# Three reorderings in a seven-stage transformer kernel: weight cracking, key tiles, and a scaling on GpSimd

## The chip, the cores and the metric

One core of a Trainium2 chip runs the whole program in one launch. TensorE (PE) multiplies matrices, VectorE (DVE) and ScalarE (ACT) do element-wise work and reductions, GpSimd (POOL) does the rest of the element-wise work, and SyncE (SP) issues the transfers. The engines run their own instruction lists in order and wait for each other through semaphores. The metric is the device time of the launch in microseconds (us), lower is better.

## What is computed

The input x is 2 batches of 1024 tokens with 256 channels, float32. Seven blocks with a residual connection follow each other; each normalises x first. Cut to what the change touches:

```python
x = x + softcap_attention(layernorm(x))       # 16 heads of 32, tanh softcap
x = x + relu_ffn(layernorm(x))                # 256 -> 512 -> 512 -> 256, the first time
x = x + plain_attention(layernorm(x))         # 16 heads of 16, 4 key heads
x = x + relu_ffn(layernorm(x))                # same weights, the second time
x = x + differential_attention(layernorm(x))  # below
x = x + gated_ffn(layernorm(x))               # weights packed as 4-bit codes with scales
x = x + test_time_training_attention(layernorm(x)); x = x + gated_ffn(layernorm(x))

# relu_ffn
x = relu(x @ W1.T + b1); x = relu(x @ W2.T + b2); out = x @ W3.T + b3
# plain_attention: causal softmax
attn = softmax(where(causal, q @ k.T / sqrt(16), min)); y = attn @ v
# differential_attention: two softmaxes, the second one scaled, and a softmax of the difference
s = softmax(where(later, -1e30, energy) / 4)
diff = where(later, -1e30, s[0] - lam * s[1]); att = softmax(diff) @ v
# unpacking of the gated feed-forward's weights
low, high = W & 15, W >> 4 & 15; W = LUT[stack(low, high)] * scales
```

## The kernel before

The stages run one after another; each of them is a function with one instruction list per engine. x (2048 tokens by 256) stays in on-chip memory. Three stages matter here.

**The small feed-forward** (`relu_ffn`, L917) runs twice, as f2 and f4, with the same weights. It works in four blocks of 512 tokens (i = 0 to 3). Float32 products are made of three products of rounded parts: each operand is held as a high part and a remainder, "low". For a block, TensorE runs `second(i)`, `first(i + 1)`, `third(i)` in this order (L1079 ff.): `first` gives the four 512-wide tiles of the first layer, `second` those of the second, `third` the output, which VectorE adds to x in `add(i)` (L1136, line L1140). ScalarE writes high parts and whole values of each tile (`relu`), and VectorE writes the remainder (`remainder`, L1128, line L1132). TensorE's `second(i)` may start only once `add(i - 1)` has emptied the accumulator bank it writes. Numbering the tiles of a block by j, tiles 0 to 3 belong to the first layer and 4 to 7 to the second.

Beside this, the stage unpacks ("cracks") the 4-bit weights of a later gated feed-forward, which have nothing to do with its own result. A part of the weights takes four VectorE steps, `crack(step)` (L955): two shifts with a mask into `f_bits` (L964, L967), an "or" into `f_code` (L971), and the multiplication by the scales into `f_weight` (L977). There are eight parts, so 32 steps, in one stage. ScalarE rounds a finished part (`keep_high`, L985), GpSimd subtracts the rounded from the whole (`keep_low`, L990), and a transfer stores it. GpSimd also adds the bias b3 to x (`add_bias`, L1011). One crack step stands behind each remainder from the third on (L1133), the last two behind the loop (L1163).

**The plain attention** (`attention` with `plain=True`, L492; tiles named ab_ and fb_) works in eight groups of one batch and four heads (g). A group has 12 steps: query block 0 (512 queries) against key tiles 0 to 3 of 128 keys, query block 1 against key tiles 0 to 7, in rising order (`steps`, L535). On the diagonal a tile needs fewer queries: tile kt of block qb is 512 wide where it lies wholly before the block, and 512, 384, 256 and 128 wide for the four diagonal tiles. `pipelined` (L402) makes the list of each engine: in slot u it issues every operation of the list with its own lag, that is for unit u - lag. On TensorE slot u holds four pieces of row scores for the running maxima (`row_piece`, L606; their widths repeat every three slots), with the scores of step u - 15 (`scores`, L634, four heads, two and two) and the weighing of the values of step u - 17 (`weigh`, L656, four heads) in between. VectorE takes the maximum of each row piece (L801); three accumulator banks rotate, so TensorE can be at most three pieces ahead. ScalarE takes the exponentials of the scores (L719), and GpSimd sets the later keys of a diagonal tile to zero (`drop_later`, L763). At the end of a group's rows the maxima are turned (`turn_maxima`, L619), split in three parts on VectorE and transferred into `fb_q_st` (L587); the scores of the group's first step wait for that transfer.

The slots of a group are named below by k = u mod 12, so the scores in slot k are those of step (k + 9) mod 12, and the weighing is that of step (k + 7) mod 12. The maxima are turned at the start of slot k = 1; the first step's scores stand in slot k = 3.

**The differential attention** (`diff_attention`, L1337; tiles named ad_) has 256 units, one for a row block of 128 queries and one head. In the 32 units of a group the row blocks t = 0 to 7 rise, four heads each, and a row of block t is (t + 1) * 128 keys wide. "Short rows" are t = 0 to 3. In slot u GpSimd issues `spread_top` of unit u - 4 (L1539), `mask` of unit u (L1522, waits for the first exponentials of unit u), and `scale_second` of unit u - 2 (L1531, waits for the coefficient of its pair of units). VectorE issues the row maxima of unit u (L1566), `mix` of unit u - 3 (L1595, waits for mask and scaling of its unit), and for every second unit the coefficients of unit u - 1.

## Time and profile before

| what | us |
|---|---|
| median of three runs | 2919.26 |
| lowest and highest of them | 2914.34, 2929.24 |
| the profiled execution's own time | 2915.69 |
| its span in the profile | 2914.0 |
| mean granted TensorE clock | 0.918 of full speed |

| stage | from, to in the span, us |
|---|---|
| first small feed-forward (f2) | 443.5 to 565 |
| plain attention (ab) | 670 to 1017 |
| second small feed-forward (f4) | 1017.5 to 1139 |
| differential attention (ad) | 1234 to 1945 |

The span is the time from the first to the last instruction of one profiled execution; what lies around it is 1.7 us. The trace gives for every instruction its start and duration, the idle time of its engine before it, and what ended that idle time. TensorE's granted clock is 1.00 at 2.4 GHz and 0.50 at 1.2 GHz. Busy times of TensorE include the latency of pipelined products, so a busy TensorE need not be at its peak.

### The profile page before, as it was taken

What the parts mean: (1) busy time and instruction counts of PE and PEld (TensorE: products, weight loads), DVE (VectorE), ACT (ScalarE), POOL (GpSimd) and SP (SyncE); (2) the same over time, 40 slices, a digit from 0 to 9 for tenths busy, and PEclk for the clock granted to TensorE, in tenths of its full rate; (3) what the DMA queues carried; (4) which work ended last, traced back from release to release, by engine and by line L of the source; (5) the groups of instructions that cost most, each with busy time, mean ns of one, the idle gap of its engine ahead of it and who ended that gap; (6) DMA issues with size and microseconds to landing.
All of it is one profiled execution on the core that took longest, in us unless ns stands there. A gap on an engine that the chain in (4) does not pass through costs nothing. (4 is left out here: it accounts for less than half of the span.)

```text
span 2914.0 us, 68812 instructions
## 1 busy us (share of the span) xinstructions
PE 2469.1 (85%) x25231; PEld 1667.2 (57%) x25320; DVE 1960.1 (67%) x4292; ACT 1710.9 (59%) x3452; POOL 856.4 (29%) x1233
## 2 busy tenths in 40 slices
PE   8887878788888788888888888878999687899998
PEld 4433336643333276445555555557888466888898
DVE  5488886667787466698888888874333355566652
ACT  2588874324454453388788788853332334677778
POOL 2244332121111121255555555520000222232223
PEclk9999888878999889999999999989999777899999
DMA  4533302244243022522140222004000658622210
GB/s 173 156 80 79 72 7 72 87 115 59 38 50 45 1 78 96 142 25 31 16 46 2 31 31 30 2 7 174 1 1 2 105 140 158 101 30 33 43 35 8
DMA packets 280879, 175.04 MB, mean 60 GB/s; under 512 B 204768, under 2 KB 241136, under 8 KB 278512
## 3 DMA queue, kind: packets, MB, share of 16 engines
q1 hardware_dynamic: 271392, 162.45, 26.7%
q10 hardware_dynamic: 9168, 8.41, 1.2%
q8 instruction: 192, 3.15, 0.5%
q14 instruction: 127, 1.04, 0.1%
HBM read 111.75 MB, written 54.66 MB: 57 GB/s over the span
## 5 line engine op out<-in xcount | busy, mean ns | idle before, releaser
L1481 ACT ACTIVATE ad_e<-ps,ad_nm 128x1024 f32<-128x1024 f32 (+7 forms) x512 | 380.2, 744 | 113.0 <-DVE ad_nm L1566 107.8
L1566 DVE TENSOR_REDUCE ad_nm<-ps 128x1 f32<-128x1024 f32 (+7 forms) x512 | 372.1, 752 | 43.8 <-PE ps L1414 31.5
L719 ACT ACTIVATE ab_e<-ps 128x512 f32<-128x512 f32 (+3 forms) x384 | 167.0, 490 | 194.9 <-PE ps L634 194.0
L1412 PE MATMUL ps<-fd_k_st,fd_q_st 96*128 96x512 bf16 (+3 forms) x768 | 215.9, 341 | 56.8 <-ACT ad_e L1481 51.2
L1595 DVE CUSTOM_DVE_ANT_0 ad_t<-ad_e,ad_rz 128x128 f32<-128x128 f32 (+7 forms) x256 | 208.2, 813 | 41.3 <-POOL ad_e L1531 24.1
L1531 POOL TENSOR_SCALAR ad_e<-ad_e,ad_c 128x128 f32<-128x128 f32 (+7 forms) x256 | 191.9, 749 | 19.3 <-DVE ad_c L1583 17.8
L1427 PE MATMUL ps<-ident,ad_t 128*128 128x128 f32 x1152 | 170.9, 276 | 26.3 <-ACT ad_prT L1491 12.7
L2007 POOL TENSOR_TENSOR st_it_low<-st_it,st_it_high 128x256 fp32r<-128x256 f32 x128 | 98.5, 783 | 315.2 <-ACT st_it_high L2270 309.7
L1491 ACT ACTIVATE ad_prT<-ps 128x128 f32<-128x128 f32 (+7 forms) x256 | 166.3, 650 | 21.4 <-PE ps L1435 21.3
L1522 POOL TENSOR_SCALAR_AFFINE_SELECT ad_e<-ad_e 128x128 f32<-128x128 f32 x256 | 90.7, 354 | 299.6 <-ACT ad_e L1481 274.4
L724 ACT ACTIVATE aa_e<-ps 128x1024 f32<-128x1024 f32 (+1 forms) x192 | 150.3, 824 | 38.0 <-PE ps L634 35.3
L840 DVE TENSOR_TENSOR aa_e_sum<-aa_e_sum,aa_e 128x2048 f32<-128x2048 f32 (+3 forms) x80 | 150.4, 1880 | 21.5 <-POOL aa_e L775 18.6
L775 POOL TENSOR_TENSOR aa_e<-aa_e,keep 128x512 f32<-128x512 f32 x64 | 108.8, 1706 | 185.4 <-ACT aa_e L731 185.2
L606 PE MATMUL ps<-fb_k_row,fb_q_row 96*128 96x512 bf16 (+3 forms) x384 | 127.4, 376 | 35.3 <-DVE ab_nm_two L801 23.8
L634 PE MATMUL ps<-fa_q_st,fa_k_st 96*128 96x512 f32 (+3 forms) x384 | 125.5, 421 | 34.1 <-ACT aa_e L724 32.3
L1427 PEld LDWEIGHTS ps<-ident,ad_t 128*128 128x128 f32 x1152 | 143.4, 143 | 17.9 <-issue 1.6
L801 DVE TENSOR_REDUCE ab_nm_two<-ps 128x1 f32<-128x512 f32 (+3 forms) x256 | 134.1, 580 | 15.7 <-PE ps L609 10.9
L731 ACT ACTIVATE aa_e<-aa_e 128x2048 f32<-128x2048 f32 (+1 forms) x96 | 143.8, 1499 | 0.0
L634 PEld LDWEIGHTS ps<-fa_q_st,fa_k_st 96*128 96x128 f32 x384 | 64.8, 207 | 137.7 <-ACT aa_e L724 83.9
L1435 PE MATMUL ps<-ad_top_diag,ad_minus 128*128 128x512 f32 (+3 forms) x384 | 133.6, 402 | 7.8 <-POOL ad_top_diag L1539 7.1
L1412 PEld LDWEIGHTS ps<-fd_k_st,fd_q_st 96*128 96x128 bf16 x768 | 56.7, 100 | 145.0 <-ACT ad_e L1481 117.0
L763 POOL TENSOR_SCALAR_AFFINE_SELECT ab_e<-ab_e 128x512 f32<-128x512 f32 x64 | 40.6, 634 | 326.9 <-ACT ab_e L719 326.9
(383 smaller groups left out, 7096.0 us busy)
## 6 DMA issues: line engine op xcount, KB each, us to landing
scr_a<-pa_parts SPq DMA_DIRECT2D x24, 512.0 KB, 2.7
fa_q_st<-scr_a SPq DMA_DIRECT2D x24, 512.0 KB, 7.8
split<-f_split SPq DMA_DIRECT2D x16, 768.0 KB, 3.9
fd_q_st<-scr_d SPq DMA_DIRECT2D x48, 256.0 KB, 8.0
g_w<-split SPq DMA_DIRECT2D x8, 1536.0 KB, 17.8
scr_d<-pd_parts SPq DMA_DIRECT2D x20, 384.0 KB, 2.8
st_w_first<-split ACTq DMA_DIRECT2D x5, 1536.0 KB, 8.1
fa_k_st<-scr_a SPq DMA_DIRECT2D x24, 256.0 KB, 8.5
```

What stands on the lines that cost most here:

```text
L634: last = pe.matmul(m.ps[:, bank, lo:QB], k_st[:, par, h // share, kt * P:(kt + 1) * P], q_st[:, par, h, qb * QB + lo:(qb + 1) * QB], start ...
L719: act.activation(e[:, u % ER, h, lo:QB], m.ps[:, n4(u, h) % 3, lo:QB], ACT.Exp, scale=scale).then_inc(s_read[0], 1)
L724: act.activation(e[:, u % ER, 2 * p:2 * p + 2, lo:QB], m.ps[:, 2 * p:2 * p + 2, lo:QB], ACT.Tanh, scale=scale / softcap).then_inc(s_read[p ...
L731: act.activation(tile, tile, ACT.Exp, scale=softcap).then_inc(exped, 1)
L840: dve.tensor_tensor(total, total, tile, ALU.add).then_inc(accrued, 1)
L1412: last = pe.matmul(m.ps[:, bank, 0:n], q_st[:, b, 2 * h + s, t * P:(t + 1) * P], k_st[:, b, s, cc * QB:cc * QB + n], start=True, stop=True)
L1427: pe.matmul(m.ps[:, bank, (kb % 4) * P:(kb % 4 + 1) * P], t2[:, u % 4, kb * P:(kb + 1) * P], m.ident[:], is_transpose=True, start=(kb % 4 ...
L1481: act.activation(e[:, u % EB, s, 0:L], src, ACT.Exp, bias=nm[:, u % EB, s:s + 1], accum_out=z[:, u % EB, s:s + 1]).then_inc(exped[s], 1)
L1491: act.activation(prT[:, u % (2 * HG), 0:L], src, ACT.Exp).then_inc(p_done, 1)
L1531: pool.tensor_scalar(e[:, k, 1, 0:L], e[:, k, 1, 0:L], c[:, k:k + 1], 1.0, ALU.mult, ALU.mult).then_inc(mixed, 1)
L1566: dve.tensor_reduce(nm[:, u % EB, s:s + 1], src, AX.X, ALU.max, negate=True).then_inc(maxed[s], 1)
L1595: dve.tensor_tensor_reduce(t2[:, u % 4, 0:L], e[:, k, 0, 0:L], e[:, k, 1, 0:L], rz[:, k, 0:1], -3.0e38, ALU.add, ALU.max, top[:, k:k + 1]) ...
```

## The change

Three edits, none of which changes the number or the size of any operation.

Feed-forward: crack steps stand behind the remainders of tiles 0, 1, 4, 5 and 6 of a block (steps 0, 1, 2, 3, 4 of the block's eight), and the other three (5, 6, 7) at the end of the block, behind the scaling of the normalisation (`norm.dve_scale`). None stands behind the remainders of tiles 2, 3 and 7.

Plain attention: `steps` takes the key tiles of a query block alternately from the front and from the back: 0, 3, 1, 2 and 0, 7, 1, 6, 2, 5, 3, 4. Counting by kt in the waits on `masked` becomes counting by `masks_to`.

Differential attention: in short rows `scale_second` stands ahead of `mask` in GpSimd's slot.

```diff
-    steps = [(qb, kt) for qb in range(T // QB) for kt in range((qb + 1) * QB // P)]
+    steps = []
+    for qb in range(T // QB):
+        tiles = range((qb + 1) * QB // P)
+        steps += [(qb, tiles[n // 2] if n % 2 == 0 else tiles[-1 - n // 2]) if plain else (qb, n) for n in tiles]
...
-    ends = {s: qb for s, (qb, kt) in enumerate(steps) if kt == (qb + 1) * QB // P - 1}
+    ends = {s: qb for s, (qb, kt) in enumerate(steps) if s + 1 == len(steps) or steps[s + 1][0] != qb}
+    masks_to = [sum(kt * P >= qb * QB for qb, kt in steps[:s + 1]) for s in range(len(steps))]
...
-                if n >= 2:
-                    crack(dve, n - 2)
+                if j in (0, 1, HT, HT + 1, HT + 2):
+                    crack(dve, 2 * HT * i + (0, 1, 0, 0, 2, 3, 4)[j])
...
-            for step in (30, 31):
-                crack(dve, step)
+                for step in range(2 * HT * i + 5, 2 * HT * i + 8):
+                    crack(dve, step)
...
-            pipelined(pool, [(4, spread_top), (0, mask), (2, scale_second)], PER, ITERS, lead=16)
+            def of_rows(short, fn):
+
+                def run(i, u):
+                    if (place(u)[2] < 4) == short:
+                        fn(i, u)
+                return run
+
+            pipelined(pool, [(4, spread_top), (2, of_rows(True, scale_second)), (0, mask), (2, of_rows(False, scale_second))],
+                      PER, ITERS, lead=16)
```

VectorE's list in f2 from the normalisation's scaling at the end of block 0 to the addition of block 0's output, before (f_h_low is a remainder, f_bits, f_code and f_weight are crack steps, x<-x,ps the addition):

```order
L146 TENSOR_SCALAR f_n_xn<-x,f_n_mv,f_n_rstd 128x256 x2
L1132 TENSOR_TENSOR f_h_low<-f_h,f_h_high 128x512
L971 TENSOR_TENSOR f_code<-f_bits 128x768
L1132 TENSOR_TENSOR f_h_low<-f_h,f_h_high 128x512
L977 SCALAR_TENSOR_TENSOR f_weight<-f_code,f_scale 128x768
L1132 TENSOR_TENSOR f_h_low<-f_h,f_h_high 128x512
L964 TENSOR_SCALAR f_bits<-f_packed 128x768
L1132 TENSOR_TENSOR f_h_low<-f_h,f_h_high 128x512
L967 TENSOR_SCALAR f_bits<-f_packed 128x768
L1140 TENSOR_TENSOR x<-x,ps 128x512 x2
```

The same place of the changed kernel:

```order
L146 TENSOR_SCALAR f_n_xn<-x,f_n_mv,f_n_rstd 128x256 x2
L971 TENSOR_SCALAR f_bits<-f_packed 128x768
L975 TENSOR_TENSOR f_code<-f_bits 128x768
L981 SCALAR_TENSOR_TENSOR f_weight<-f_code,f_scale 128x768
L1136 TENSOR_TENSOR f_h_low<-f_h,f_h_high 128x512
L968 TENSOR_SCALAR f_bits<-f_packed 128x768
L1136 TENSOR_TENSOR f_h_low<-f_h,f_h_high 128x512
L971 TENSOR_SCALAR f_bits<-f_packed 128x768
L1136 TENSOR_TENSOR f_h_low<-f_h,f_h_high 128x512 x2
L1144 TENSOR_TENSOR x<-x,ps 128x512 x2
```

Three crack steps stand behind the scaling and ahead of the first remainder, and two behind the first two remainders; the crack step that stood ahead of the scaling (behind the remainder of tile 7) is gone from there.

TensorE's list in the loop of the plain attention, slot k = 3 from the group's first scores on, before (L634 scores, L606 and L609 row pieces, L656 the weighing):

```order
L634 MATMUL ps<-fb_q_st,fb_k_st 128x512
L428 REGISTER_ALU
L634 MATMUL ps<-fb_q_st,fb_k_st 128x512
L428 REGISTER_ALU
L606 MATMUL ps<-fb_k_row,fb_q_row 128x384
L609 MATMUL ps<-later_k,ident_b 128x128
L428 REGISTER_ALU
L656 MATMUL ps<-ab_e,ab_v_st 32x256 x4
```

The same place of the changed kernel:

```order
L638 MATMUL ps<-fb_q_st,fb_k_st 128x512
L428 REGISTER_ALU
L638 MATMUL ps<-fb_q_st,fb_k_st 128x512
L428 REGISTER_ALU
L610 MATMUL ps<-fb_k_row,fb_q_row 128x384
L613 MATMUL ps<-later_k,ident_b 128x128
L660 MATMUL ps<-ab_e,ab_v_st 32x512 x4
```

The weighing in this slot, which follows the wait for the transferred maxima, is 512 wide instead of 256. The widths of scores and weighing in all twelve slots are, before and after:

| slot k | 0 | 1 | 2 | 3 | 4 | 5 | 6 | 7 | 8 | 9 | 10 | 11 |
|---|---|---|---|---|---|---|---|---|---|---|---|---|
| scores before | 384 | 256 | 128 | 512 | 384 | 256 | 128 | 512 | 512 | 512 | 512 | 512 |
| scores after | 384 | 512 | 512 | 512 | 128 | 384 | 256 | 512 | 128 | 512 | 256 | 512 |
| weighing before | 512 | 512 | 384 | 256 | 128 | 512 | 384 | 256 | 128 | 512 | 512 | 512 |
| weighing after | 256 | 512 | 384 | 512 | 512 | 512 | 128 | 384 | 256 | 512 | 128 | 512 |

GpSimd's list in the differential attention, two slots of short rows, before (L1539 `spread_top`, L1522 `mask`, L1531 `scale_second`):

```order
L1539 TENSOR_SCALAR ad_top_diag<-ident,ad_top 128x128
L1522 AFFINE_SELECT ad_e<-ad_e 128x128
L1531 TENSOR_SCALAR ad_e<-ad_e,ad_c 128x256
L1539 TENSOR_SCALAR ad_top_diag<-ident,ad_top 128x128
L1522 AFFINE_SELECT ad_e<-ad_e 128x128
L1531 TENSOR_SCALAR ad_e<-ad_e,ad_c 128x256
```

The changed kernel there:

```order
L1543 TENSOR_SCALAR ad_top_diag<-ident,ad_top 128x128
L1535 TENSOR_SCALAR ad_e<-ad_e,ad_c 128x256
L1526 AFFINE_SELECT ad_e<-ad_e 128x128
L1543 TENSOR_SCALAR ad_top_diag<-ident,ad_top 128x128
L1535 TENSOR_SCALAR ad_e<-ad_e,ad_c 128x256
L1526 AFFINE_SELECT ad_e<-ad_e 128x128
```

Within a slot the scaling of unit u - 2 and the mask of unit u have changed places; `spread_top` stays first.

## Rows read from the trace of the kernel before

**Rows 1.** The page's first line.

```profile
span 2914.0 us, 68812 instructions
```

**Rows 2.** Stages f2, ab and ad: length, busy us of each engine, clock, DMA share, GB/s.

```profile
443.50:565.00 121.50, 102.28 (x512) 86.49 (x512) 77.95 (x130) 56.10 (x93) 33.05 (x24) 0.90 0.24 80
670.00:1017.00 347.00, 293.17 (x1854) 117.60 (x1852) 254.23 (x476) 173.57 (x400) 40.61 (x64) 0.93 0.30 40
...
1234.00:1945.00 711.00, 577.47 (x5351) 358.35 (x5440) 599.71 (x1425) 570.82 (x1416) 369.29 (x770) 0.97 0.19 23
```

**Rows 3.** Who waited for the addition L1140: us in total, times.

```profile
  PE ps L1035: 13.0, 4
```

**Rows 4.** VectorE by time, end of block 0 in f2: start, us, what, [idle before].

```profile
472.96 0.95 DVE L967 TENSOR_SCALAR f_bits<-f_packed 128x768 int32<-128x768 int32 x1
...
476.49 0.69 DVE L1132 TENSOR_TENSOR f_h_low<-f_h,f_h_high 128x512 fp32r<-128x512 f32 x1 [1.66 <-ACT f_h L1106]
...
478.38 1.94 DVE L1132 TENSOR_TENSOR f_h_low<-f_h,f_h_high 128x512 fp32r<-128x512 f32 x1 [0.33 <-ACT f_h L1106]
480.24 1.50 DVE L977 SCALAR_TENSOR_TENSOR f_weight<-f_code,f_scale 128x768 f32<-128x768 fp8e4 x1
...
485.48 1.27 DVE L1140 TENSOR_TENSOR x<-x,ps 128x512 f32<-128x512 f32 x2
```

**Rows 5.** TensorE by time at the same place.

```profile
481.90 1.04 PE L176 MATMUL ps<-ident,f_n_xn 128*128 128x128 f32 x8
486.21 0.79 PE L1035 MATMUL ps<-f_h_high,ffn_high 128*128 128x512 f32 x1 [3.27 <-DVE x L1140]
```

**Rows 6.** GpSimd by time at the same place.

```profile
477.26 2.50 POOL L990 TENSOR_TENSOR f_split<-f_weight,f_split 128x768 fp32r<-128x768 f32 x1 [21.48 <-ACT f_split L985]
479.72 4.43 POOL L1011 TENSOR_TENSOR x<-x,f_b 128x256 f32<-128x256 f32 x4
```

**Rows 7.** Stretches at half clock behind the four waits: the first, and the sum.

```profile
485.88:489.29 3.41, 3.08 (x7) 2.48 (x8) 2.07 (x4) 0.00 (x0) 0.00 (x0) 0.50 0.03 5
...
sum 20.47, PE 18.21 PEld 14.40 DVE 8.72 ACT 0.55 POOL 0.00; mean PE 4.55 PEld 3.60 DVE 2.18 ACT 0.14 POOL 0.00
```

**Rows 8.** The load of the scales, both stages: issue ns, first and last start; landing.

```profile
L943 SPq DMA_DIRECT2D f_scale<-in_scales x2: 620/621/622, 445.5 to 1019.6; - x2
...
DMA to landing us min/median/max: 11.4/11.6/11.8
```

**Rows 9.** TensorE by time in the plain attention, slots k = 1 and k = 3 of a group.

```profile
835.99 1.07 PE L656 MATMUL ps<-ab_e,ab_v_st 128*32 128x512 f32 x8
...
842.89 0.59 PE L634 MATMUL ps<-fb_q_st,fb_k_st 99*128 99x512 bf16 x2 [1.11 <-issue]
...
843.63 0.64 PE L656 MATMUL ps<-ab_e,ab_v_st 128*32 128x256 f32 x8
```

**Rows 10.** VectorE by time in the plain attention: slots k = 9, 0, 1, 3.

```profile
821.99 0.69 DVE L801 TENSOR_REDUCE ab_nm<-ps 128x1 f32<-128x512 f32 x1 [0.93 <-PE ps L609]
...
833.34 0.69 DVE L801 TENSOR_REDUCE ab_nm<-ps 128x1 f32<-128x512 f32 x1 [0.65 <-PE ps L609]
...
837.59 0.42 DVE L801 TENSOR_REDUCE ab_nm_two<-ps 128x1 f32<-128x256 f32 x1 [0.56 <-PE ps L609]
...
845.78 0.69 DVE L801 TENSOR_REDUCE ab_nm<-ps 128x1 f32<-128x512 f32 x1 [1.48 <-PE ps L609]
```

**Rows 11.** Stretch behind the wait of slot k = 3, columns as in rows 2.

```profile
844.30:847.60 3.30, 3.30 (x16) 1.27 (x17) 1.60 (x4) 2.04 (x5) 0.64 (x1) 0.50 1.05 129
```

**Rows 12.** Who waited for the scaling L1531: us in total, times.

```profile
  DVE ad_t L1595: 24.1, 34
```

**Rows 13.** VectorE and GpSimd by time, short rows of the differential attention.

```profile
1513.50 0.62 DVE L1595 CUSTOM_DVE_ANT_0 ad_t<-ad_e,ad_rz 128x384 f32<-128x384 f32 x1
...
1520.87 0.62 DVE L1595 CUSTOM_DVE_ANT_0 ad_t<-ad_e,ad_rz 128x384 f32<-128x384 f32 x1 [0.55 <-POOL ad_e L1531]
...
1513.29 0.37 POOL L1539 TENSOR_SCALAR ad_top_diag<-ident,ad_top 128x128 fp32r<-128x128 f32 x1
```

More of the change, by code:

```diff
@@ L649, in weigh @@
                 if kt * P >= qb * QB:
-                    wait(pe, masked, i, 2 * BT, g * BT + kt + 1)
+                    wait(pe, masked, i, 2 * BT, g * BT + masks_to[s])
                 if s == 0:
@@ L832, in accrue @@
                 if kt * P >= qb * QB:
-                    wait(dve, masked, i, 2 * BT, g * BT + kt + 1)
+                    wait(dve, masked, i, 2 * BT, g * BT + masks_to[s])
                 total, tile = e_sum[:, qb % 2, :, lo:QB], e[:, u % ER, :, lo:QB]
```

## The prediction

> **What bounds the kernel now.** I read the page's span first [rows 1]: 2914.0 us, and 1.7 us more in the execution's own time of 2915.69, which is 3.6 below the median of the three runs. Then the busy time by stage [rows 2]. No engine fills a stage: in f2 TensorE is busy for 102 of 121.5 us and VectorE for 86, in ab TensorE for 293 and VectorE for 254 of 347, in ad TensorE for 577, VectorE for 600 and GpSimd for 571 of 711. So each stage is held by waits between engines, and an edit is worth what it does to them. The three edits touch different stages and I price them apart.
>
> In the feed-forward the view of what waits for one line is the one to look at: TensorE waits for the addition L1140 four times, 13.0 us in all [rows 3], and those are all its long waits there. The lists by time show how one arises (end of block 0 in f2, the other three are alike). TensorE ends its work at 481.90 + 1.04 = 482.94 and starts `second(1)` at 486.21, after 3.27 us [rows 5]. VectorE, whose addition it waits for, had ended the norm's scaling at 476.49 - 1.66 = 474.83, stood idle for 1.66, and then did four remainders and four crack steps up to the addition at 485.48 [rows 4]. These are slow: a remainder takes 0.69 and once 1.94, and `f_weight` 1.50, while GpSimd runs its subtraction (2.50) and its bias additions (4.43) [rows 6]. Behind the wait TensorE's granted clock is 0.50, that is 1.2 GHz, for 3.41 us here and for 20.47 us behind all four, with TensorE busy for 18.21 of them [rows 7].
>
> In the attention I read by slot. TensorE and VectorE hand row pieces on, and VectorE waits for TensorE in slots k = 9, 0, 1 and 3 (0.93, 0.65, 0.56, 1.48) [rows 10]; the last follows the wait of TensorE for the transferred maxima (1.11) [rows 9]. In the other slots it is VectorE that sets the pace.
>
> **The feed-forward edit.** The number of steps is the same, their places differ. It does three things to the stretch in front of the addition. The crack step behind tile 7 (0.95 [rows 4]) goes from ahead of the scaling, so the scaling ends at 473.88. Three steps then stand behind the scaling, where VectorE was idle for 1.66; at 0.95 each, the price of `f_bits`, they end at 476.73, 0.24 after the first remainder could have started. And two steps remain between the remainders where there were four: `f_code` and `f_weight` go, at least 0.95 + 1.50 = 2.45, so 2.45 - 0.24 = 2.2 us come free. Not all of it reaches the addition: the 0.33 for which VectorE waited for ScalarE [rows 4] can return, and GpSimd's subtraction starts when it did (477.26), so one of the remainders still meets it and is stretched. Laid out: first remainder to 477.4, `f_bits` to 478.4, second remainder to 480.3 as before, `f_bits` to 481.3, two remainders of 0.7 to 1.2 each to 483.3, or up to half a us later if a bias addition stands in the way. The addition then starts some 1.7 us earlier, at 483.8, and the wait falls from 3.27 to about 1.6. The bounds are 0 (the stretching by GpSimd eats all) and 3.27 (no wait is left). Four times 1.7 are 6.8 us. In the last block there is no scaling and no wait to hide in: three crack steps stand ahead of the last addition where two did, less what was stretched, some 0.4 for each stage, +0.8.
>
> Second term, the clock: at half speed 18.21 us of busy TensorE cost up to 9.1 us. A wait half as long may or may not keep the clock up. The 1.11 in the attention [rows 9] is shorter than the 1.6 that I expect, and behind it too TensorE runs at 0.50 [rows 11]. So it is open, and I take half, -4.5, with the ends 0 and -9.1. The load of the scales: it is issued at 445.5 and lands at most 11.8 later [rows 8], at 457.3; the first crack step that needs it now stands early in the first block, and waits for nothing more than some tenths, so 0. The rest of the unpacking (ScalarE's rounding, GpSimd's subtraction, the store) keeps its order; a part's `f_weight` is ready at the end of the block and not two remainders later, at no cost. Sum -10.5 us, bounds -22 and 0.
>
> What holds GpSimd and VectorE apart matters for this: the Trainium skill ("SBUF — State Buffer", section "Who interferes with whom") says that a VectorE instruction with two on-chip inputs and a GpSimd instruction that reads that memory exclude each other for the whole of an instruction. The trace agrees in f2, where `f_bits` with one input stays at 0.95 and the remainder goes to 1.94 [rows 4]. By that rule alone the remainders keep their stretch wherever the crack steps go.
>
> **The attention edit.** The tiles of a group are the same, so TensorE's sum is unchanged; it moves between slots. The price: weighing of 512 columns takes 1.07 and of 256 takes 0.64 [rows 9], so 0.21 for 128 columns; two score products of 512 take 0.59, and I price scores at the same 0.21 for 128 columns of four heads. From the table of widths: slot k = 0 loses 0.43, 1 gains 0.43, 2 gains 0.64, 3 gains 0.43, 4 and 5 gain 0.21 each, 6 loses and 7 gains 0.21, 8 loses 0.43, 10 loses 1.07; the sum is nothing. What counts is where VectorE waits for TensorE. Slot 8's loss shortens the wait in k = 9 (0.93) by 0.43, slot 0's that of k = 0 (0.65) by 0.43. Against it stand 0.43 in k = 1, which delays the turning of the maxima, and 0.43 in k = 3. The 0.64 in k = 2 lies in the time in which TensorE waits for the split and the transfer anyway, its 1.11 of [rows 9] being the last of those waits. Slots 4 and 5 add up to 0.42, 6, 7 and 10 lie where VectorE sets the pace. So a group costs between 0 and 0.4. I take 0.2 for seven groups, +1.5, plus the end of the stage, where the last weighing is 512 wide and not 128: 3 x 0.21 = 0.6. Against it the fuller slot 2 leaves TensorE less idle ahead of the stretch where its clock is down, which I put at -1. Sum +1; bounds -6 (no half clock left behind k = 3) and +10 (below).
>
> **The differential edit.** Only `mix` needs the scaling, and it waited for it 34 times, 24.1 us [rows 12]. By the lists that is mostly at long rows, which don't change, and of the length of a signal; in short rows a few units of a group wait longer, such as the 0.55 at 1520.87 [rows 13]. With the scaling a mask earlier these shrink by up to the mask's length. The mask itself comes later, but only `mix` three slots on reads it. At most 5 us sits in such waits of short rows; VectorE, busy for 600 of 711 us, will give part of it back at its next wait. I take -3, bounds -6 and +4.
>
> GpSimd's operations beside `mix` don't stretch it in the trace: at 1513.29 `spread_top` (0.37) has begun and `mix` at 1513.50 still takes 0.62, as it does alone at 1520.87 [rows 13]. The section of the Trainium skill named above would have it otherwise, since `mix` reads two halves of a tile: then moving the scaling next to `mix` blocks it. That is the last rival.
>
> **The sum** is -10.5 + 1 - 3 = -12.5 us, 2903.2 against the execution's own 2915.7, and 2907 against the median.
>
> **Rivals.** (1) The wait closes wholly, and the clock stays up: 13.0 + 9.1 are 22, less 0.8, with +1 and -3 -24, so 2895. For it: 2.2 us come free at known prices and the clock falls only behind the wait. Against: 2.2 is less than 3.27. (2) The edits do little. GpSimd's subtraction and bias additions last from 477.26 to 484.15 [rows 6], and the remainders wait for these and not for the crack steps; the addition starts nearly when it did. Then some -2 us are left, 2917. Against it: two of the steps that go were not idle time but 2.45 us of work. (3) Slower: the attention's k = 1 to 5 carry 0.43 + 0.64 + 0.43 + 0.21 + 0.21 = 1.92 us more and nothing of it is hidden, since VectorE's list has run dry when the maxima are turned; 3 to 5, at half clock, cost twice, so 2.8 a group and 22 over eight, from the point on where the losses in k = 8 to 0 meet a VectorE that is already at its own pace. With +1 and -10.5 that is +12.5, 2932. (4) Slower: the scaling, moved ahead of the mask, meets `mix` and holds it for its own 0.37 in half of 128 short units: +24, and with the rest +14, 2934. Against: [rows 13].
>
> **Chances.** Forecast 0.45, (1) 0.2, (2) 0.25, (3) 0.06, (4) 0.04. The predicted time is the forecast's. The range runs from 2892, under rival (1), to 2922, over rival (2), and leaves out (3), (4) and some of both tails. A measurement can tell about 0.5% (14.6 us) from no change. That is 2904.7: rival (1) and somewhat under half of the forecast lie below, 0.4; above 2933.9 a part of (3) and (4), 0.05; within 0.55.
>
> **What would show it.** Step by step: TensorE's wait for the addition in f2 and f4 falls from 13.0 to about 6 (rival 1: 0, rival 2: over 11); the stretches at half clock there from 20.5 to some 10; each of the two stages from 121.5 to about 119. In VectorE's list three crack steps stand where the 1.66 was, and the addition starts near 483.8. In the attention the waits of VectorE in k = 9 and 0 fall by 0.4 and those in k = 1 and 3 rise by 0.4, and the stage stays within 1 or 2 of 347; rival (3) would show up to 370. In the differential stage `mix` waits for the scaling for about 20 in place of 24.1, `mix` keeps its 0.62, and 711 becomes 708; 0.9 in place of 0.62 would be rival (4). The prediction is wrong if the attention's stage moves by more than 6 in either direction, since I had that as near balance, or if the first two remainders are stretched by more than the one subtraction.

## The result, and the profile after

The changed kernel takes 2887.1 us in the median of 4 runs (2880.74 to 2896.34), the kernel before 2917.31 in the median of its 4. The ratio is 0.9883 with a 95% interval of 0.9856 to 0.9909: 1.2% faster, 30 us between the medians. The forecast was 2907 in a range of 2892 to 2922; the time lies below it. Between the two profiled executions the span falls from 2914.0 [rows 1] to 2879.2, by 34.8.

The page's first line, and the three stages of [rows 2] in the changed kernel (length, then busy time of TensorE, its weight loads, VectorE, ScalarE and GpSimd, clock, DMA share, GB/s):

```profile
span 2879.2 us, 68812 instructions
```

```profile
442.85:556.85 114.00, 98.93 (x512) 83.92 (x512) 77.77 (x130) 56.76 (x93) 30.52 (x24) 0.92 0.25 85
662.70:1007.80 345.10, 289.09 (x1854) 114.55 (x1852) 250.68 (x476) 173.54 (x400) 40.77 (x64) 0.95 0.30 40
1216.40:1910.60 694.20, 568.09 (x5351) 356.58 (x5440) 597.77 (x1425) 571.48 (x1416) 377.77 (x770) 0.98 0.20 24
```

f2 is 7.5 us shorter, the plain attention 1.9, f4 8.5 and the differential attention 16.8 (711.0 to 694.2). That is 34.7 of the 34.8. The forecast had -10.5 for f2 and f4 together (measured -16.0), +1 for the plain attention (-1.9) and -3 for the differential one (-16.8).

**Feed-forward.** The view of who waited for the addition, both stages (us, times); in [rows 3] it was 13.0 in 4:

```profile
  PE ps L1039: 4.4, 4
```

VectorE, TensorE and GpSimd by time at the end of block 0 in f2, where [rows 4 to 6] show the kernel before (start, us, what, idle before):

```profile
473.27 0.73 DVE L146 TENSOR_SCALAR f_n_xn<-x,f_n_mv,f_n_rstd 128x256 f32<-128x256 f32 x2
473.91 0.95 DVE L971 TENSOR_SCALAR f_bits<-f_packed 128x768 int32<-128x768 int32 x1
474.89 0.96 DVE L975 TENSOR_TENSOR f_code<-f_bits 128x768 int32<-128x768 int32 x1
475.89 0.96 DVE L981 SCALAR_TENSOR_TENSOR f_weight<-f_code,f_scale 128x768 f32<-128x768 fp8e4 x1
476.76 2.33 DVE L1136 TENSOR_TENSOR f_h_low<-f_h,f_h_high 128x512 fp32r<-128x512 f32 x1
479.02 0.94 DVE L968 TENSOR_SCALAR f_bits<-f_packed 128x768 int32<-128x768 int32 x1
479.88 1.07 DVE L1136 TENSOR_TENSOR f_h_low<-f_h,f_h_high 128x512 fp32r<-128x512 f32 x1
480.88 0.94 DVE L971 TENSOR_SCALAR f_bits<-f_packed 128x768 int32<-128x768 int32 x1
481.74 1.66 DVE L1136 TENSOR_TENSOR f_h_low<-f_h,f_h_high 128x512 fp32r<-128x512 f32 x2
483.32 1.27 DVE L1144 TENSOR_TENSOR x<-x,ps 128x512 f32<-128x512 f32 x2
```

```profile
481.93 1.04 PE L176 MATMUL ps<-ident,f_n_xn 128*128 128x128 f32 x8
484.05 0.50 PE L1039 MATMUL ps<-f_h_high,ffn_high 128*128 128x512 f32 x1 [1.08 <-DVE x L1144]
```

```profile
476.44 2.12 POOL L994 TENSOR_TENSOR f_split<-f_weight,f_split 128x768 fp32r<-128x768 f32 x1 [21.27 <-ACT f_split L989]
478.51 3.74 POOL L1015 TENSOR_TENSOR x<-x,f_b 128x256 f32<-128x256 f32 x4
```

The three crack steps fill what was 1.66 us of idle time, and each takes 0.95 or 0.96. One remainder (2.33) meets GpSimd's subtraction. The addition starts at 483.32 and TensorE waits 1.08. The first product behind the wait takes 0.50, where it took 0.79 [rows 5]. The clock behind the first wait, and in the last block (columns as above):

```profile
484.10:487.40 3.30, 3.30 (x14) 2.69 (x15) 1.69 (x3) 0.19 (x1) 0.00 (x0) 1.00 0.02 5
544.80:548.10 3.30, 3.30 (x15) 3.30 (x16) 3.16 (x3) 0.00 (x0) 1.82 (x1) 0.50 0.07 25
```

The stretches at half clock behind the four waits [rows 7] are gone. A single one stands in f2's last block, behind a wait of 2.08 us for a remainder which both kernels have; before there was one in each of the two last blocks. These cost the stage nothing, since its end hangs on something else. SyncE stores the last cracked part and then begins the next stage; at the end of f2 in the kernel before:

```profile
559.47 0.51 SPq L1025 DMA_DIRECT2D split<-f_split  x1
564.47 0.39 SPq L215 DMA_DIRECT2D pb_w<-in_wqk_b  x1
```

The last remainder starts at 552.19; three crack steps, ScalarE's rounding, GpSimd's subtraction and this store follow, and the next stage begins 12.3 us behind the remainder. In the changed kernel it is 12.3 too, in f2 with a half-clock stretch and in f4 without one.

**Differential attention.** The groups of `mix` by width, before and after. The number behind the second bar is VectorE's idle time ahead of them. Before:

```profile
L1595 DVE CUSTOM_DVE_ANT_0 ad_t<-ad_e,ad_rz 128x1024 f32<-128x1024 f32 x32 | 41.0, 1283 | 22.7 <-POOL ad_e L1531 15.4 <-issue 7.3
L1595 DVE CUSTOM_DVE_ANT_0 ad_t<-ad_e,ad_rz 128x896 f32<-128x896 f32 x32 | 36.6, 1143 | 0.0
...
L1595 DVE CUSTOM_DVE_ANT_0 ad_t<-ad_e,ad_rz 128x512 f32<-128x512 f32 x32 | 23.9, 746 | 0.2
...
L1595 DVE CUSTOM_DVE_ANT_0 ad_t<-ad_e,ad_rz 128x384 f32<-128x384 f32 x32 | 19.7, 616 | 8.5 <-issue 4.4 <-POOL ad_e L1531 3.6
L1595 DVE CUSTOM_DVE_ANT_0 ad_t<-ad_e,ad_rz 128x256 f32<-128x256 f32 x32 | 15.5, 484 | 5.7 <-POOL ad_e L1531 2.9 <-issue 1.2
L1595 DVE CUSTOM_DVE_ANT_0 ad_t<-ad_e,ad_rz 128x128 f32<-128x128 f32 x32 | 11.2, 350 | 4.1 <-POOL ad_e L1531 2.2 <-issue 1.8
```

After:

```profile
L1607 DVE CUSTOM_DVE_ANT_0 ad_t<-ad_e,ad_rz 128x1024 f32<-128x1024 f32 x32 | 41.0, 1282 | 22.9 <-POOL ad_e L1535 15.6 <-issue 7.3
...
L1607 DVE CUSTOM_DVE_ANT_0 ad_t<-ad_e,ad_rz 128x384 f32<-128x384 f32 x32 | 22.0, 688 | 0.3
L1607 DVE CUSTOM_DVE_ANT_0 ad_t<-ad_e,ad_rz 128x256 f32<-128x256 f32 x32 | 16.0, 499 | 0.2 <-issue 0.2
L1607 DVE CUSTOM_DVE_ANT_0 ad_t<-ad_e,ad_rz 128x128 f32<-128x128 f32 x32 | 11.5, 359 | 3.0 <-POOL ad_e L1535 2.2 <-issue 0.7
```

Ahead of `mix` in short rows VectorE stood idle for 0.2 + 8.5 + 5.7 + 4.1 = 18.5 us, and now for 3.5. That is 15.0 less. `mix` of 384 has grown from 616 to 688 ns, and all widths together by 3.5 us (208.2 to 211.7). For the whole stage VectorE's idle time falls by 14.9 (111.3 to 96.4, the length less the busy time) and its busy time by 1.9 (599.7 to 597.8), in spite of the longer `mix`; together they are the 16.8. Which instructions account for the 1.9 is not shown. The groups of 1024, which wait at the turn of a group of units, are as they were.

One such wait before, first GpSimd and then VectorE by time:

```profile
1514.89 0.29 POOL L1522 TENSOR_SCALAR_AFFINE_SELECT ad_e<-ad_e 128x128 f32<-128x128 f32 x1 [1.23 <-ACT ad_e L1481]
1515.17 0.58 POOL L1531 TENSOR_SCALAR ad_e<-ad_e,ad_c 128x384 f32<-128x384 f32 x1
```

```profile
1515.94 0.62 DVE L1595 CUSTOM_DVE_ANT_0 ad_t<-ad_e,ad_rz 128x384 f32<-128x384 f32 x1 [0.74 <-issue]
```

GpSimd stands idle for 1.23 us because the mask of the newest unit waits for ScalarE. Only then comes the scaling, whose coefficient VectorE had finished at 1512.52, and `mix` starts 0.19 us after its end. The view names no engine for this wait ("issue"), though it is the scaling's.

**Plain attention.** Length of the slots k = 0 to 11 of the group that begins at 785.9 us before, from VectorE's row maxima, in us:

| slot k | 0 | 1 | 2 | 3 | 4 | 5 | 6 | 7 | 8 | 9 | 10 | 11 |
|---|---|---|---|---|---|---|---|---|---|---|---|---|
| before | 3.06 | 4.18 | 3.96 | 5.76 | 2.22 | 3.04 | 3.61 | 4.13 | 3.31 | 3.54 | 3.66 | 4.66 |
| after | 2.64 | 4.60 | 3.57 | 5.99 | 2.29 | 2.95 | 3.61 | 4.13 | 3.31 | 3.24 | 3.66 | 4.66 |

Slots 0 and 1 move by 0.42 down and up, as priced at 0.43, slot 9 by 0.3 down, slot 3 by 0.23 up. The slots that VectorE paces (6 to 8, 10, 11) don't move. The group is 0.5 us shorter in all.

### The profile page after: what moved, and what is told of

The parts are those of the page before. It is cut to its first block and busy times, and to the rows that moved or that the text cites. A ratio compares the mean times of both kernels' runs of the same rounds, so it can differ in the third digit from the quotient of the medians.

```text
span 2879.2 us, 68812 instructions
## 1 busy us (share of the span) xinstructions
PE 2442.1 (85%) x25231; PEld 1648.5 (57%) x25320; DVE 1953.5 (68%) x4292; ACT 1712.7 (59%) x3452; POOL 857.1 (30%) x1233
## 5 line engine op out<-in xcount | busy, mean ns | idle before, releaser
L1535 POOL TENSOR_SCALAR ad_e<-ad_e,ad_c 128x128 f32<-128x128 f32 (+7 forms) x256 | 197.9, 773 | 82.9 <-DVE ad_c L1595 80.9
L844 DVE TENSOR_TENSOR aa_e_sum<-aa_e_sum,aa_e 128x2048 f32<-128x2048 f32 (+3 forms) x80 | 151.3, 1891 | 21.3 <-POOL aa_e L779 18.6
L1526 POOL TENSOR_SCALAR_AFFINE_SELECT ad_e<-ad_e 128x128 f32<-128x128 f32 x256 | 83.2, 325 | 210.8 <-ACT ad_e L1485 187.5
## 6 DMA issues: line engine op xcount, KB each, us to landing
g_w<-split SPq DMA_DIRECT2D x8, 1536.0 KB, 17.8
```

The lines of the kernel that those rows point to most:

```text
L844: dve.tensor_tensor(total, total, tile, ALU.add).then_inc(accrued, 1)
L1535: pool.tensor_scalar(e[:, k, 1, 0:L], e[:, k, 1, 0:L], c[:, k:k + 1], 1.0, ALU.mult, ALU.mult).then_inc(mixed, 1)
```

## Experiments

The table holds what each kernel's own profiled execution lost (-) or gained (+) in a stage against that of the kernel before, in us, and the measured ratio to the kernel before. A stage in which two kernels don't differ still varies: the differential attention by up to 2, f2 and f4 by up to 0.5 without the edit and 1.4 with it. The last stage of the program, which none of them touches, varied from -5 to +14, so that the stage lengths tell more than the sums.

| kernel | f2 | plain attention | f4 | differential | ratio, 95% |
|---|---|---|---|---|---|
| changed kernel | -7.5 | -1.9 | -8.5 | -16.8 | 0.9883 (0.9856 to 0.9909) |
| e1_ffn | -7.5 | -1.9 | -8.5 | +0.2 | 0.9947 (0.9925 to 0.9970) |
| e2_keys | -0.1 | -3.5 | 0.0 | -1.5 | 0.9996 (0.9977 to 1.0015) |
| e3_scale | 0.0 | +0.2 | +0.1 | -17.0 | 0.9937 (0.9905 to 0.9970) |
| e4_warm | -3.9 | +0.1 | -4.0 | +1.6 | 0.9976 (0.9955 to 0.9997) |
| e5_late_mask | -0.5 | +2.3 | -0.5 | +0.8 | 1.0010 (0.9982 to 1.0038) |
| e6_all_first | -8.1 | -2.6 | -7.3 | -0.2 | 0.9926 (0.9898 to 0.9954) |
| e7_two_behind | -8.3 | +1.3 | -8.5 | +1.5 | 0.9960 (0.9936 to 0.9983) |
| e8_four_behind | -6.8 | -0.1 | -7.2 | -0.7 | 0.9968 (0.9945 to 0.9992) |
| e9_no_keys | -8.2 | -2.6 | -7.1 | -17.1 | 0.9898 (0.9866 to 0.9929) |
| e10_short_late_mask | 0.0 | +0.7 | +0.2 | -15.0 | 0.9948 (0.9926 to 0.9971) |
| e11_three_places | -8.3 | -1.9 | -8.5 | -18.9 | 0.9864 (0.9835 to 0.9893) |

### Each edit alone

The first three kernels are the kernel before with one of the three parts of the diff each.

Feed-forward alone:

> The feed-forward edit alone on the kernel before. Theory (the edits act apart, and in the feed-forward the clock is won as well as the wait): stages f2 and f4 together 16 us shorter than before (in the trace after they are 7.5 and 8.5 shorter), TensorE's wait for the addition L1140 near 5 us where it was 13, no stretch of half clock behind it, about 2901 us in all. Rival (half of the forecast's clock term, the rest came with the other edits): 8 to 10 us, 2907.

Measured: -16.0 in f2 and f4, TensorE's wait for the addition 4.5 us, the clock at 1.00 behind it. The theory holds; the gain is the edit's own.

Order of the key tiles alone:

> The order of the key tiles alone. Theory (the edits act apart): the stage of the plain attention 1.9 us shorter, as in the trace after, with half-clock stretches of 3.4 us in every group where every second one was 6.8; in all 2915, not to be told from before. Rival (the order costs time, and the two other edits hid it by the phase in which they hand over): the stage 0.5 to 5 us longer.

Measured: 3.5 us shorter in the stage, and nothing that a measurement can tell in all. The shorter half-clock stretches, on which the expectation rested, are no property of the order: in `e1_ffn`, with the old order, they are 3.4 us in every group too.

Scaling ahead of the mask in short rows alone:

> The scaling ahead of the mask in short rows, alone. Theory (the whole of it is mix of short rows, which no longer waits for a scaling that stood behind the mask's wait for ScalarE): the stage of the differential attention 16.7 us shorter as in the trace after, idle time of VectorE ahead of mix in short rows from 14 us to about zero, in all 2900. Rival (what was gained in that stage came from the clock or from where the earlier stages left off): 3 to 6 us, 2912.

Measured: -17.0 in the stage, ratio 0.9937. The theory holds. The three ratios multiplied give 0.9880, and the changed kernel has 0.9883: the edits act apart.

### What the clock is worth in the feed-forward

The clock falls behind the wait, so both were gone at once in the changed kernel. This run takes the clock alone: the wait stays, and is filled with products that nobody uses.

```diff
             for i in range(NB):
+                if i in (1, 2):
+                    pe.wait_ge(whole, 2 * HT * i + 1)
+                    keep_warm(pe, m, 0, 14)
                 second(i)
```

> The kernel before with 14 more 512-wide products of constants on TensorE ahead of the second layer of blocks 1 and 2, in an accumulator bank that is free there: they fill the wait for the addition and change nothing else. Theory (the half clock is the consequence of the wait, and costs about as much as the time at half clock times one half): the waits stay, filled, the clock stays at 1.00 behind them, and f2 and f4 together are 8 to 9 us shorter than before. Rival (the clock falls for another reason, or the products at half clock are not what ends the stage): 0 to 3 us.

TensorE by time at the end of block 0 in f2, and the clock behind the first of the four waits (L435 are the added products):

```profile
483.46 1.03 PE L176 MATMUL ps<-ident,f_n_xn 128*128 128x128 f32 x8
484.33 3.19 PE L435 MATMUL ps<-warm,ident_b 128*128 128x512 bf16 x14
487.75 0.50 PE L1035 MATMUL ps<-f_h_high,ffn_high 128*128 128x512 f32 x1 [0.23 <-DVE x L1143]
```

```profile
488.00:491.30 3.30, 3.30 (x15) 2.67 (x15) 1.49 (x3) 0.40 (x1) 0.00 (x0) 1.00 0.02 5
```

The second layer starts no earlier, 487.75 - 484.49 = 3.26 us behind the end of the transposes, and yet f2 and f4 are 3.9 + 4.0 = 7.9 us shorter. The clock is 1.00 behind all four. The half clock was a consequence of the idle time and cost some 8 us. The stretches in the two last blocks are gone too in this run, which by the 12.3 us above is worth nothing to the stages. With the wait's own 13.0 - 4.4 = 8.6 this makes 16.5, and the two stages gained 16.0: all of it, within what they vary by.

### What sets the length of the wait

The number of crack steps behind the scaling is three in the changed kernel. Two runs change it, with the rest of the kernel as before. In all three there are five crack steps between the scaling and the addition; what changes is how many of them stand ahead of the first remainder:

```diff
-                if n >= 2:
-                    crack(dve, n - 2)
+                if j in (0, 1, 2, 4, 5, 6):
+                    crack(dve, 2 * HT * i + {0: 0, 1: 1, 2: 2, 4: 3, 5: 4, 6: 5}[j])
...
-            for step in (30, 31):
-                crack(dve, step)
+                for step in range(2 * HT * i + 6, 2 * HT * i + 8):
+                    crack(dve, step)
```

> The kernel before, with only two crack steps behind the scaling of a block and three behind the remainders of tiles 0, 1 and 2 (one more ahead of the addition than in the changed kernel). Theory: TensorE's wait for the addition is about 0.95 longer than the 1.1 to 1.4 of the changed kernel, 2.1 to 2.3 us, which costs 4 us over f2 and f4. If the clock falls only behind a wait as long as the old 3.27, the two stages are 12 us shorter than before; if it falls behind 2.2 too, 4 to 5 us shorter. I lean to the second, since in the plain attention it falls behind 1.11. Rival: the steps meet GpSimd otherwise and the wait is as in the changed kernel, 16 us shorter.

```diff
-                if n >= 2:
-                    crack(dve, n - 2)
+                if j in (0, 4, 5, 6):
+                    crack(dve, 2 * HT * i + {0: 0, 4: 1, 5: 2, 6: 3}[j])
...
-            for step in (30, 31):
-                crack(dve, step)
+                for step in range(2 * HT * i + 4, 2 * HT * i + 8):
+                    crack(dve, step)
```

> The kernel before, with four crack steps behind the scaling of a block and one behind the first remainder. Theory (what stands between scaling and addition sets the wait, one step is worth 0.95): the wait for the addition falls to 0.1 to 0.5, f2 and f4 18 to 20 us shorter than before, 2 to 4 more than with the changed kernel's places. Rival (the first remainder, blocked by GpSimd's subtraction, and those behind it set it now, so the step only moves the blockade): 15 to 16 us, as in the changed kernel.

Both theories fell. Of the rivals, the first came true (f2 and f4 are 16.8 us shorter); the second named the subtraction, but its 15 to 16 us were 14.0. At the end of block 0 in f2, VectorE, GpSimd and TensorE by time in the run with two steps:

```profile
478.40 0.68 DVE L1132 TENSOR_TENSOR f_h_low<-f_h,f_h_high 128x512 fp32r<-128x512 f32 x1
...
480.18 1.28 DVE L1132 TENSOR_TENSOR f_h_low<-f_h,f_h_high 128x512 fp32r<-128x512 f32 x1 [0.23 <-ACT f_h L1106]
```

```profile
479.07 1.85 POOL L990 TENSOR_TENSOR f_split<-f_weight,f_split 128x768 fp32r<-128x768 f32 x1 [21.17 <-ACT f_split L985]
```

```profile
486.52 0.50 PE L1035 MATMUL ps<-f_h_high,ffn_high 128*128 128x512 f32 x1 [0.92 <-DVE x L1140]
```

The same in the run with four, with TensorE's clock behind the wait:

```profile
475.68 2.49 DVE L977 SCALAR_TENSOR_TENSOR f_weight<-f_code,f_scale 128x768 f32<-128x768 fp8e4 x1
478.09 1.22 DVE L1132 TENSOR_TENSOR f_h_low<-f_h,f_h_high 128x512 fp32r<-128x512 f32 x1
```

```profile
475.36 1.99 POOL L990 TENSOR_TENSOR f_split<-f_weight,f_split 128x768 fp32r<-128x768 f32 x1 [20.31 <-ACT f_split L985]
```

```profile
483.57 0.50 PE L1035 MATMUL ps<-f_h_high,ffn_high 128*128 128x512 f32 x1 [1.67 <-DVE x L1140]
```

```profile
483.70:487.00 3.30, 3.30 (x15) 2.67 (x16) 1.61 (x3) 0.27 (x1) 0.00 (x0) 1.00 0.02 5
```

With two steps the wait for the addition is 0.92, with three 1.08, with four 1.67. Moving one more step into the idle time ahead of the first remainder doesn't shorten the wait by its 0.95; it lengthens it. What differs in the lists is what meets the subtraction. With two, the first remainder is through before the subtraction starts, and the second meets only its end (1.28). With three, the first remainder meets all of it (2.33). With four, `f_weight` does (2.49) and a remainder behind it goes to 1.22. Behind none of these waits does the clock fall; behind 3.27 it did. The run with two has a wait of 0.51 for a remainder in one place more, and comes to -16.8 for both stages, against -16.0 in the changed kernel. Behind its last remainder stand two crack steps and not three, and the next stage begins 11.9 us behind it and not 12.3: that can be the 0.8 of both stages, which is no larger than the scatter.

The thirteen traces together give a count for these two stages. In or behind the 20 waits for the addition of 3.23 to 3.28 us the clock fell each time. Behind the 28 of 0.91 to 1.67 it never did. Behind the wait of 2.08 in the last block, which every kernel has, it fell in 14 cases of 26.

The length of the idle time alone doesn't decide about the clock. TensorE in the 2.30 us ahead of the 1.11 in the plain attention behind which the clock falls [rows 9, 11], and ahead of the 3.27 in f2:

```profile
839.48:841.78 2.30, 1.08 (x6) 0.34 (x6) 2.30 (x5) 0.40 (x2) 0.63 (x1) 1.00 0.04 7
480.60:482.90 2.30, 2.30 (x21) 2.10 (x19) 2.30 (x3) 0.80 (x2) 2.30 (x3) 1.00 0.81 278
```

In the attention TensorE had been busy for 1.08 of 2.30 us when the 1.11 came, in f2 for all of them. That this is why the short wait sufficed there is likely; no run changes it by itself.

### What held the scaling in short rows

> The kernel before, GpSimd's mask one slot later (of unit u - 1 in slot u), scaling still behind it, in all rows. Mix reads the mask two slots later still. Theory (the scaling of short rows was held by the mask's wait for ScalarE's exponentials of the newest unit, not by the mask's 0.29 to 0.35 us): the same waits of mix go as with the scaling ahead of the mask, the stage of the differential attention 15 us or more shorter than before. Rival (the mask's own length and the memory it shares with VectorE held the scaling): the scaling still starts a mask later, 2 to 6 us shorter.

```diff
-            pipelined(pool, [(4, spread_top), (0, mask), (2, scale_second)], PER, ITERS, lead=16)
+            pipelined(pool, [(4, spread_top), (1, mask), (2, scale_second)], PER, ITERS, lead=16)
```

And the changed kernel with its order in all rows:

> The changed kernel with the scaling ahead of the mask in all rows, not the short ones alone. Theory (long rows have no wait of mix for the scaling but at the turn of a group, where the last units wait 0.63, 1.17 and 1.06 us, and there the mask delays one of three): the stage 5 to 8 us shorter than in the changed kernel. Rival (in long rows the scaling of 0.8 to 1.2 us now lies beside mix and the two hold each other up, and the mask comes too late): the stage 5 to 20 us longer.

```diff
-            pipelined(pool, [(4, spread_top), (2, of_rows(True, scale_second)), (0, mask), (2, of_rows(False, scale_second))],
-                      PER, ITERS, lead=16)
+            pipelined(pool, [(4, spread_top), (2, scale_second), (0, mask)], PER, ITERS, lead=16)
```

Neither stage is shorter than before (+0.8 and -0.2). The groups of `mix` by width in `e6_all_first`:

```profile
L1599 DVE CUSTOM_DVE_ANT_0 ad_t<-ad_e,ad_rz 128x1024 f32<-128x1024 f32 x32 | 46.3, 1448 | 14.5 <-POOL ad_e L1535 13.3 <-issue 1.2
L1599 DVE CUSTOM_DVE_ANT_0 ad_t<-ad_e,ad_rz 128x896 f32<-128x896 f32 x32 | 44.7, 1397 | 0.0
...
L1599 DVE CUSTOM_DVE_ANT_0 ad_t<-ad_e,ad_rz 128x640 f32<-128x640 f32 x32 | 32.4, 1014 | 0.0
...
L1599 DVE CUSTOM_DVE_ANT_0 ad_t<-ad_e,ad_rz 128x384 f32<-128x384 f32 x32 | 22.0, 687 | 0.3
```

The idle time of short rows is gone here too, and that of the widest falls from 22.7 to 14.5: over all eight widths the idle time ahead of `mix` falls by 23.5 us (41.3 to 17.8). But `mix` itself grows by 26.0 (208.2 to 234.2). It is the long rows: 1448 for 1283 ns, 1397 for 1143. In `e5_late_mask` the figures are 1439 and 1420, so the order of mask and scaling is not what does it; both kernels let the scaling of a long row start early, beside `mix`. Two units of one group in `e6_all_first`, and the scaling that stands beside the first (the last line):

```profile
1286.26 1.57 DVE L1599 CUSTOM_DVE_ANT_0 ad_t<-ad_e,ad_rz 128x896 f32<-128x896 f32 x1
1290.03 1.13 DVE L1599 CUSTOM_DVE_ANT_0 ad_t<-ad_e,ad_rz 128x896 f32<-128x896 f32 x1
...
1285.88 1.02 POOL L1535 TENSOR_SCALAR ad_e<-ad_e,ad_c 128x896 f32<-128x896 f32 x1
```

0.64 us of the scaling were left when the first `mix` began, and it takes 0.44 longer than the second, which has nothing of GpSimd beside it. One more run puts this to the test: the mask late in short rows only.

```diff
-            pipelined(pool, [(4, spread_top), (0, mask), (2, scale_second)], PER, ITERS, lead=16)
+            pipelined(pool, [(4, spread_top), (1, of_rows(True, mask)), (0, of_rows(False, mask)), (2, scale_second)],
+                      PER, ITERS, lead=16)
```

> The kernel before, GpSimd's mask one slot later in short rows only, long rows as before; the scaling stands behind the mask. The late mask in all rows took the waits of mix in short rows away and gave the time back in long rows, where mix grew from 208 to 233 us in all. Theory (short rows gain because the scaling no longer stands behind a mask that waits for ScalarE; long rows lose because a scaling that is early meets mix): the stage 14 to 17 us shorter than before, mix at 208 to 212 us in all. Rival (the gain needs the scaling ahead of the mask, and a late mask costs what it brings elsewhere): 0 to 6 us shorter.

The same groups in `e10_short_late_mask`:

```profile
L1603 DVE CUSTOM_DVE_ANT_0 ad_t<-ad_e,ad_rz 128x896 f32<-128x896 f32 x32 | 36.5, 1142 | 0.0
...
L1603 DVE CUSTOM_DVE_ANT_0 ad_t<-ad_e,ad_rz 128x384 f32<-128x384 f32 x32 | 21.9, 684 | 0.4
```

The stage is 15.0 us shorter, with the scaling still behind the mask, and `mix` takes 210.7 us in all. So what held the scaling was the mask's wait for ScalarE and not its length, and the limit to short rows is what keeps the gain: in long rows the wait of the mask had kept the scaling out of the way of `mix`.

### The changed kernel without the key order, and with other places for the crack steps

`e9_no_keys` is the feed-forward and the scaling part of the diff without the one on key tiles. `e11_three_places` is the changed kernel with the places of `e7_two_behind`.

> The changed kernel without the new order of key tiles. Theory (that order moves time between slots and changes no sum): the same time as the changed kernel within 4 us, ratio to before 0.988 to 0.990; the stage of the plain attention 0 to 3.5 us longer than with the new order. Rival (the order is worth something only together with the others, or costs): 5 us or more apart.

> The changed kernel with the crack steps in the places of the run with two steps behind the scaling (tiles 0, 1, 2, 4, 5, 6, and two behind the scaling), whose wait for the addition was 0.92 where the changed kernel has 1.1. Theory: f2 and f4 together 0.5 to 1 us shorter than in the changed kernel, in all 0 to 1 us, which a measurement can't tell. Rival (the 0.51 for which TensorE waited for a remainder there costs it): 0 to 1 us longer.

Without the new order the ratio is 0.9898, with it 0.9883, and their intervals share 0.9866 to 0.9909. In the stage's length the four kernels that have it show -1.9 to -3.5 (mean -2.5), the eight others -2.6 to +2.3 (mean 0). A gain of some 2 us is likely and not settled. What goes with it is the clock: between the stage's first 50 us and its last 20, TensorE is at half clock for 17 to 21 us in the four, and for 24 to 38 us in the kernel before and the eight others. But the two of the others with the least (24 and 27 us) are 1.9 and 2.6 us shorter as well, without the new order. `e11_three_places` has the lowest time, 2884.07 in the median of 5, ratio 0.9864; it can't be told from the changed kernel.

## Why the prediction was wrong

The profiled executions differ by 34.8 us where the sum had 12.5. Of the 22.3 that are missing, 13.8 are the differential attention's, 5.5 the feed-forward's and 2.9 the plain attention's. With the differential attention at its -16.8 and all else as forecast, the time would have been 2893, inside the range.

**What bounds the kernel.** Waits between engines in three stages, priced apart: right, as the three runs of one edit each show.

**The wait in the feed-forward**, from 3.27 to about 1.6, 6.8 us in all. The mechanism is as told, and the layout too: three steps in the idle time, one remainder stretched by the subtraction, two later ones slightly. The size was off by the half us that was kept back "if a bias addition stands in the way": the addition starts at 483.32 where 483.8 was written, and the wait is 1.08 to 1.15. It gave 8.6 us. The +0.8 for the last block was a miscount: it has three crack steps ahead of the last addition "where two did", but before, step 29 stood behind the last remainder as well, so that from its tile 4 on the last block has the same list in both kernels. And these four were not "all its long waits": TensorE also waits 2.08 for a remainder in each last block, and 6.17 for the normalisation at the start of each stage. What was not seen is how the wait depends on the steps. The prediction priced a crack step at its 0.95; the runs with two and four behind the scaling show that the meeting with the subtraction outweighs it.

**The clock**, -4.5 as the half of 9.1. It was all or nothing, and it was all: 7.9 us, measured alone. A half of an event that comes wholly or not at all is a mean of two outcomes and itself neither of them. The row taken as evidence against (the clock falls behind 1.11 in the attention) was of a stretch in which TensorE had been half idle before. What TensorE did ahead of both waits was there to be read.

**The plain attention**, +1. Right in part: slots 0 and 1 by 0.42, slot 9 by 0.3 for 0.43, slot 3 by 0.23 for 0.43, nothing where VectorE sets the pace. But slots 4 and 5, priced at +0.42 together, stay the same, and slot 2 is 0.4 shorter where nothing was expected. So the sign was wrong: the group shown is 0.5 shorter where 0.2 longer was taken. The stage's -1.9 lies within the bounds and within what it varies by.

**The differential attention**, -3. This is the step that failed: "At most 5 us sits in such waits of short rows." It was 18.5, and 15.0 of them went. The mechanism, a `mix` that no longer waits for a late scaling, was right, and the term was far too small. It was also priced by the mask's length, 0.29, where what stood in the way was the mask's wait for ScalarE, such as the 1.23 above, as `e10_short_late_mask` shows. The waits were taken from the row of those attributed to the scaling [rows 12], which was then put down to long rows. In the view of groups by width, the 24.1 are 15.4 at 1024 and 8.7 in short rows, and beside them stand 14.7 us of waits of the same instruction which the trace calls "issue", 7.4 of them in short rows. A wait of 0.74 as at 1515.94 is one of these. Its neighbour was quoted [rows 13] as one of "a few units of a group"; but short rows are 128 of the 256 units, and 18.5 us are 0.14 for each of them. The back-payment at VectorE's next wait, also in that step, didn't come: its idle time ahead of the row maxima stayed the same within 0.4 us.

Neither of the two signs that the prediction named for being wrong came up, and neither stood in this stage: no rival had more than the forecast to gain there.

**The rivals.** (1), 2895 with -24, was nearest, by luck in part: its gain over the forecast was all in the feed-forward, where the -16.0 lies midway between its -21.3 and the forecast's -10.5. The clock went its way, the wait (1.1 left) the forecast's. (3), a slower attention, has nothing for it, and its sum was off too: 22 - 10.5 - 3 is +8.5 and not +12.5. (4) was refused for [rows 13], an overlap of 0.16 us. In the example from `e6_all_first` 0.64 of overlap stretch `mix` by 0.44, that is 0.2 less, so 0.16 could show nothing. The mechanism is real. In short rows `mix` of 384 grew from 616 to 688 ns in the changed kernel, which the gained idle time outweighs; in long rows, in the two runs that let the scaling come early there, it cost all of the gain. The Trainium skill ("SBUF — State Buffer", section "Who interferes with whom") has a VectorE instruction with two on-chip inputs and a GpSimd instruction that reads that memory exclude each other. The traces agree: `mix` of 896 takes 1397 for 1143 ns where the scaling stands beside it, and in the list after, the remainder with its two inputs takes 2.33 beside the subtraction while `f_bits` with one stays at 0.94 beside the bias addition.

## To carry to other kernels

A wait that comes in a few places of a loop is read as a sum over the loop, grouped by shape, and with the time that the trace attributes to nobody: of the 18.5 us here 7.4 stood under "issue". An instruction that waits for a fresh result shouldn't stand ahead of one that is ready, in an engine that works in order; but ask what the early one will then lie beside. Where TensorE stands idle and its clock falls behind that, the wait is worth more than its length: here 8.6 us of waiting and 7.9 more for the 20.5 us at the lower clock. And before a stage's last block is counted, look at what the next stage waits for: here it was a store that had nothing to do with the stage's own result.

## What was not expected of the hardware

Idle times of TensorE of 0.91 to 1.67 us in the feed-forward left its clock at 1.00 in 28 cases of 28, 3.23 to 3.28 brought it to 0.50 in 20 of 20, and 2.08 in 14 of 26; and 1.11 did so in the attention, where TensorE had been busy for 1.08 of the 2.30 us before. Fourteen unused products in each of the four waits kept it at 1.00, and the two stages got 7.9 us shorter.

The same crack step `f_weight` took 0.96 us where it began ahead of GpSimd's subtraction (475.89, the subtraction at 476.44) and 2.49 where it began behind it (475.68 and 475.36). `mix` of 896 columns took 1143 ns in the mean, and 1397 with the scaling beside it.
